# A new static order of steps for the five engines in the Layers phase of an attention and feed-forward kernel

## The reference, cut to what matters

```
h = shift_token(x)                      # half of the features come from the token before
q, k, v = split(h @ wqkv)               # 8 heads of 64
q, k = rotary_xpos(l2norm(q) * qs, l2norm(k) * ksc)
o = softmax(q k^T * 8, own and previous window of 128 keys, causal) v
x = x + o @ wo
h = layernorm(shift_token(x)) * lg + lb
a, g = split(h @ w1 + b1);  x = x + (a * gelu(g)) @ w2 + b2
```

## Time and profile before

| | before |
|---|---|
| median of three runs | 3927.06 us |
| the profiled execution | 3927.97 us |
| its span, first to last instruction | 3926.1 us |
| PE busy | 3360.0 us (86%) |
| DVE busy | 2846.7 us (73%) |
| ACT busy | 2352.7 us (60%) |
| POOL busy | 1511.6 us (39%) |
| mean granted TensorE clock | 0.953 of full speed |

### The profile page before, as it was taken

One profiled execution on the slowest core, in us unless ns is written; L12 is line 12 of the kernel. 1 busy time (PEld: TensorE's weight loads), 2 busy tenths in 40 slices (PEclk: granted clock), 3 DMA queues, 4 the chain that ended last, 5 costly groups with the idle time before them and its releaser, 6 DMA issues.

```text
span 3926.1 us, 77200 instructions
## 1 busy us (share of the span) xinstructions
PE 3360.0 (86%) x29600; PEld 1960.8 (50%) x29600; DVE 2846.7 (73%) x4121; ACT 2352.7 (60%) x2813; POOL 1511.6 (39%) x1171
## 2 busy tenths in 40 slices
PE   2888888888855799998999989878999899998998
PEld 1223232323223566565666666545656666665665
DVE  4778787777745777777777776667877777777764
ACT  0566666565643566666656666555666666666654
POOL 1212121212104445455444554443545544455443
PEclk7999999999987899999999999988999999999999
DMA  2222222222211000000000001010010100101000
GB/s 56 49 61 54 60 53 60 52 60 52 51 50 39 15 20 19 27 19 29 19 20 26 25 23 36 30 44 24 25 32 24 35 29 24 32 29 36 24 27 30
DMA packets 149008, 139.11 MB, mean 35 GB/s; under 512 B 11132, under 2 KB 147376, under 8 KB 148912
## 3 DMA queue, kind: packets, MB, share of 16 engines
q1 hardware_dynamic: 148912, 137.78, 13.4%
HBM read 70.40 MB, written 33.55 MB: 26 GB/s over the span
## 4 chain that ended last, share of the span: by engine, by line
PE 35%; DVE 15%; ACT 11%; issue 7%; POOL 1%; DMA 1%; SPq 0%; DVEq 0%; ACTq 0%; POOLq 0%
PE f_p L1026 13%; PE f_p L1162 7%; DVE f_Ph L1374 6%; PE f_p L1133 5%; PE f_p L1052 3%; PE f_p L1043 3%; ACT f_Ph L1253 2%; ACT f_Pl L1245 2%; DVE f_xh L1456 2%; PE f_p L1059 2%; ACT f_hT L1274 1%; DVE f_rt L248 1%; ACT f_gates L1268 1%; DVE f_xT_l L1343 1%; PE f_p L1008 1%
## 5 line engine op out<-in xcount | busy, mean ns | idle before, releaser
L654 DVE TENSOR_REDUCE m_negm<-m_p 128x2 f16<-128x1024 f32 x512 | 608.7, 1222 | 169.2 <-PE m_p L473 167.5
L576 ACT ACTIVATE m_Pr<-m_p 128x1024 f32<-128x1024 f32 x512 | 500.4, 1020 | 164.0 <-PE m_p L492 159.6
L1374 DVE TENSOR_TENSOR f_Ph<-f_Pl,f_Ph 128x896 f16<-128x896 f32 x256 | 377.0, 1514 | 213.3 <-ACT f_Ph L1253 213.3
L1540 POOL TENSOR_TENSOR f_u<-f_u,f_bt 128x1024 f32<-128x1024 f32 x128 | 301.8, 2358 | 465.6 <-DVE f_bt L1359 465.6
L1556 POOL TENSOR_TENSOR f_hT<-f_gates,f_hT 128x512 f16<-128x512 f32 x192 | 234.2, 1223 | 587.9 <-ACT f_gates L1276 587.6
L1268 ACT ACTIVATE f_gates<-f_p,f_bias 128x512 f32<-128x512 f32 x192 | 131.4, 684 | 469.0 <-PE f_p L1162 469.0
L501 PE MATMUL m_o<-m_Pr,m_vm 128*32 128x512 f32 x2048 | 341.6, 646 | 13.0 <-ACT m_Pr L576 13.0
L1026 PE MATMUL f_p<-f_wq_h,f_xT_h 128*128 128x512 f16 x768 | 307.0, 400 | 26.1 <-DVE f_xhT_l L1462 12.7
L1545 POOL TENSOR_TENSOR f_u<-f_u,f_rn 128x1024 f32<-128x1024 f32 x128 | 289.1, 2258 | 74.3 <-DVE f_mark_v L1387 74.3
L1392 DVE TENSOR_REDUCE f_negm<-f_p 128x4 bf16<-128x1024 f32 x256 | 300.8, 1222 | 17.0 <-PE f_p L1059 16.6
L1026 PE MATMUL f_p<-f_wq_l,f_xT_h 128*128 128x512 f16 x768 | 305.3, 398 | 0.0
(11 more groups left out here) (235 smaller groups left out, 8540.8 us busy)
## 6 DMA issues: line engine op xcount, KB each, us to landing
f_xs<-out SPq DMA_DIRECT2D x32, 512.0 KB, 4.4
f_xr<-out SPq DMA_DIRECT2D x32, 512.0 KB, 5.0
out<-f_xb SPq DMA_DIRECT2D x32, 512.0 KB, 3.0
m_xin<-in_L_attn_x SPq DMA_DIRECT2D x16, 512.0 KB, 4.1
out<-m_xn SPq DMA_DIRECT2D x16, 512.0 KB, 3.0
m_QT<-m_hi SPq DMA_DIRECT2D x128, 64.0 KB
m_KT<-m_hi SPq DMA_DIRECT2D x128, 64.0 KB
m_xr<-in_L_attn_x SPq DMA_DIRECT2D x16, 512.0 KB, 4.7
```

The source lines that it names most:

```text
L576: act.activation(Pr[kt % 2][:, 2 * u:2 * u + 2, :].rearrange("p h t -> p (h t)"), psum[w.slot("M2", g, kt, u)][:, :], ACT.Exp).then_inc(*w ...
L654: dve.tensor_reduce(negm[:, t, pr // 2, :, pr % 2], psum[w.slot("M1", h, u)][:, :].rearrange("p (a k) -> p a k", a=2), AX.X, ALU.max, nega ...
L1374: dve.tensor_tensor(Pp[h % 4][:, 1, :], Pl[h % 2][:], Pp[h % 4][:, 0, :], ALU.subtract).then_inc(*p_lo_ready.up(I))
L1540: pool.tensor_tensor(u[t][:], u[t][:], bt[:], ALU.add).then_inc(*bt_used.up(I))
```

## The change

The change rewrites the table and nothing else: every engine has the instructions that it had, SP's queue stays the same, and PE's, ACT's, DVE's and POOL's steps are in another order.

```diff
     order = {
-        "PE": """... C.ST,3 A.QK,3 D.WO,0 C.L1,0
-               D.WO,1 D.WO,2 D.WO,3 C.L1,1 F.W1,0 ...
+        "PE": """... C.ST,3 A.QK,3 C.L1,0 D.WO,0
+               D.WO,1 D.WO,2 D.WO,3 C.L1,1 F.W1,0 ...
         "ACT":
-               F.H1,0 F.W1,2 F.H1,1 F.W1,3 C.LM F.H1,2 F.W1,4 F.H1,3 F.W1,5 F.H1,4 F.H1,5 C.L2,0 C.PH,0 ...
+               F.H1,0 F.W1,2 F.H1,1 F.W1,3 F.H1,2 C.LM F.W1,4 F.H1,3 F.W1,5 F.H1,4 C.L2,0 F.H1,5 C.PH,0 ...
         "DVE":
-               ... A.QK,2 A.QK,3 D.WO,0 D.WO,1 D.WO,2 C.L1,0 D.WO,3 C.L1,1
-               F.W1,0 C.L1,2 F.W1,1 C.L1,3 C.LM F.W1,2 A.RN F.W1,3 F.W1,4 F.W1,5 F.ZB N.LN F.W2,0 C.PL,0 C.PL,1 F.W2,1 F.W2,2 N.LA
-               C.PL,2 C.PV,0 C.PL,3 C.PV,1 N.XH C.PV,2 C.PV,3""",
+               ... A.QK,2 C.L1,0 A.QK,3 D.WO,0 D.WO,1 D.WO,2 D.WO,3 C.L1,1
+               F.W1,0 C.L1,2 F.W1,1 C.L1,3 F.W1,2 C.LM F.W1,3 N.LN F.W1,4 A.RN F.W1,5 F.ZB F.W2,0 F.W2,1 C.PL,0 C.PL,1 F.W2,2 N.LA
+               C.PL,2 C.PV,0 C.PV,1 C.PL,3 N.XH C.PV,2 C.PV,3""",
-        "POOL": """A.QK,0 ... A.QK,3 F.H1,0 F.H1,1 F.H1,2 F.H1,3 F.H1,4 F.H1,5 A.NM,0 N.LR A.SQ,0 A.SH,0 A.NM,1 ... A.NM,3 A.SQ,3 A.SH,3 N.LS""",
+        "POOL": """A.QK,0 A.QK,1 A.QK,2 F.H1,0 F.H1,1 A.QK,3 F.H1,2 F.H1,3 A.NM,0 F.H1,4 F.H1,5 N.LR A.SQ,0 A.SH,0 A.NM,1 ... A.NM,3 N.LS A.SQ,3 A.SH,3""",
```

More of the change, by code:

```diff
@@ L798, in layers_phase @@
     order = {
-        "PE": """C.V,0 C.V,1 C.V,2 C.V,3 A.XT C.ST,0 D.OT,0 D.OT,1 A.QK,0 C.ST,1 A.QK,1 C.ST,2 A.QK,2 C.ST,3 A.QK,3 D.WO,0 C.L1,0
+        "PE": """C.V,0 C.V,1 C.V,2 C.V,3 A.XT C.ST,0 D.OT,0 D.OT,1 A.QK,0 C.ST,1 A.QK,1 C.ST,2 A.QK,2 C.ST,3 A.QK,3 C.L1,0 D.WO,0
                D.WO,1 D.WO,2 D.WO,3 C.L1,1 F.W1,0 C.L1,2 F.W1,1 C.L1,3 F.W1,2 F.W1,3 C.LM F.W1,4 F.W1,5 C.L2,0 F.W2,0 F.W2,1 C.L2,1
@@ L802, in layers_phase @@
         "ACT": """C.V,0 C.V,1 C.V,2 C.V,3 A.XT C.ST,0 D.OT,0 D.OT,1 A.QK,0 C.ST,1 A.QK,1 C.ST,2 A.QK,2 C.ST,3 A.QK,3 F.W1,0 F.W1,1
-               F.H1,0 F.W1,2 F.H1,1 F.W1,3 C.LM F.H1,2 F.W1,4 F.H1,3 F.W1,5 F.H1,4 F.H1,5 C.L2,0 C.PH,0 A.HI,0 C.L2,1 C.PH,1 C.L2,2
+               F.H1,0 F.W1,2 F.H1,1 F.W1,3 F.H1,2 C.LM F.W1,4 F.H1,3 F.W1,5 F.H1,4 C.L2,0 F.H1,5 C.PH,0 A.HI,0 C.L2,1 C.PH,1 C.L2,2
                C.PH,2 A.HI,1 C.L2,3 C.PH,3 N.XH A.HI,2 A.HI,3""",
-        "DVE": """C.V,0 C.V,1 C.V,2 C.V,3 A.XT D.OT,0 D.OT,1 A.QK,0 A.QK,1 A.QK,2 A.QK,3 D.WO,0 D.WO,1 D.WO,2 C.L1,0 D.WO,3 C.L1,1
-               F.W1,0 C.L1,2 F.W1,1 C.L1,3 C.LM F.W1,2 A.RN F.W1,3 F.W1,4 F.W1,5 F.ZB N.LN F.W2,0 C.PL,0 C.PL,1 F.W2,1 F.W2,2 N.LA
-               C.PL,2 C.PV,0 C.PL,3 C.PV,1 N.XH C.PV,2 C.PV,3""",
-        "POOL": """A.QK,0 A.QK,1 A.QK,2 A.QK,3 F.H1,0 F.H1,1 F.H1,2 F.H1,3 F.H1,4 F.H1,5 A.NM,0 N.LR A.SQ,0 A.SH,0 A.NM,1 A.SQ,1 A.SH,1
-               A.NM,2 A.SQ,2 A.SH,2 A.NM,3 A.SQ,3 A.SH,3 N.LS""",
-        "SP": """A.XT N.LX C.XR F.W2,0 F.W2,1 F.W2,2 N.XH""",
+        "DVE": """C.V,0 C.V,1 C.V,2 C.V,3 A.XT D.OT,0 D.OT,1 A.QK,0 A.QK,1 A.QK,2 C.L1,0 A.QK,3 D.WO,0 D.WO,1 D.WO,2 D.WO,3 C.L1,1
+               F.W1,0 C.L1,2 F.W1,1 C.L1,3 F.W1,2 C.LM F.W1,3 N.LN F.W1,4 A.RN F.W1,5 F.ZB F.W2,0 F.W2,1 C.PL,0 C.PL,1 F.W2,2 N.LA
+               C.PL,2 C.PV,0 C.PV,1 C.PL,3 N.XH C.PV,2 C.PV,3""",
+        "POOL": """A.QK,0 A.QK,1 A.QK,2 F.H1,0 F.H1,1 A.QK,3 F.H1,2 F.H1,3 A.NM,0 F.H1,4 F.H1,5 N.LR A.SQ,0 A.SH,0 A.NM,1 A.SQ,1 A.SH,1
+               A.NM,2 A.SQ,2 A.SH,2 A.NM,3 N.LS A.SQ,3 A.SH,3""",
+        "SP": """A.XT F.W2,0 N.LX C.XR F.W2,1 F.W2,2 N.XH""",
     }
```

## The result

| | before | changed |
|---|---|---|
| median of the runs | 3926.84 us | 3965.28 us (3958.99 to 3968.09) |
| ratio to before, with its interval | | 1.0097 [1.0081, 1.0113] |
| span of the profiled execution | 3926.1 us | 3963.0 us |
| PE busy | 3360.0 us | 3382.9 us |
| mean granted clock of TensorE | 0.953 | 0.941 |

A forecast was written before the change was run, and what follows sets the result against it. PE was taken as the bound, busy 74.48 of 81 us in a round. Over 13 loop rounds per layer, +0.2 (layer 0) and +1.0 (layer 1) sum to 15.6 us on 3927.1: 3943 us, range 3908 to 3975.

The forecast's parts named there:

- the likeliest case: Whole kernel: the prediction's own forecast, 3935 to 3955 us, chance 0.35.
- The unrolled rounds I take at 0: Rounds outside the two 13-round loops: no change in time, 0 us.
- the front: Round's start: `L1,0` before `WO,0` on PE, before `QK,3` and `WO` on DVE; cost 0.
- The clock, -0.2 per round: Turn of the round: low-clock stretch stays put and half the delay within it is given back, -0.2 us.
- rival D: PE's waits before the turn: clock falls more often or longer, 22 us, 3965 us; chance 0.12.
- `V,0` behind `PV,3`, +0.72: Round's end: next round's `V,0` waits for `PV,3`'s division instead of `XH`'s drain, +0.72 us per round.
- the last pair: Last two `PL` instructions of a round on DVE: in layer 0 end 0.3 us earlier, still split by `NM,2`.
- Layer 0's path, +0.42: Layer 0 loop rounds before the clock term: last `PL` pair -0.3 and `V,0` +0.72 us per round.
- Layer 1, +1.22 before the clock: Layer 1 loop rounds: `ZB` kept out, delaying the last `PL` pair +0.5 us, plus `V,0` +0.72.
- The waits of 0.55 and 1.45: PE's waits before `L2,0` and `L2,3`: the 0.55 us goes, the 1.45 us shrinks.
- PE's busy time should not change: PE over the whole kernel: same instructions, so busy time stays the same.

The follow-up runs named there:

- e3: Changed kernel with only `LN` put back behind `W1,5` and `ZB` on DVE: 3946.13 us, ratio 1.0050.
- e8: Kernel before with only `LN` moved forward on DVE, to behind `W1,3`: 3962.52 us, ratio 1.0086.
- e5: Changed kernel with `PV,2` given PSUM slot p0 and `PV,3` the other one: 3952.26 us, ratio 1.0060.
- e17: Changed kernel with 8 extra matmuls on PE ahead of `PV,2`: 3948.49 us, ratio 1.0052.
- e13: Kernel before with 16 extra matmuls on PE ahead of `PV,2`: 3911.12 us, ratio 0.9957.
- e6: Changed kernel with the front and `LN` both put back to their old order: 3907.34 us, ratio 0.9943.
- e12: Kernel before with `LN` early; meant to move `W2`'s drain too, but no instruction moved, so e8 repeated: 3962.52 us, ratio 1.0088.
- e15: Kernel before with `LN` early and 16 extra matmuls on PE ahead of `PV,2`: 3949.92 us, ratio 1.0053.
- e18: Kernel before with the new front alone and 16 extra matmuls on PE ahead of `PV,2`: 3976.88 us, ratio 1.0128.

## Why the prediction was right and wrong

Slower was forecast, and slower it is. 3965 lies between 3908 and 3975, but not in the 3935 to 3955 of the likeliest case: the change is 38 us where 16 were forecast. Point by point, the step that failed first:

- **"The unrolled rounds I take at 0": the step that failed.** They lost 13.7 us. The prediction's walk through the round gave `LN` nothing, neither its own time nor a wait: `RN`, which now stands behind it, was forecast at 2072.2, +18.7 of the round, and starts at +20.5. It took `LN`'s inputs as ready. The copy of `x1` takes some 16 us from its issue; `LN` used to come some 20 us after it, and now comes before it has landed. Outside the loops the waits for it are 16.5 us instead of 2.5, and PE passes them on (10.54 and 4.58 at `W2`). In the loops 26 of them, 50.5 us in all, make no round longer beside the new front (e3: 81.91 and 81.92 without them), though the chain that ended last in the changed kernel gives this copy 11% of the span. e3, which gives back 19 us, shows that `LN`'s place is the cause. That it is the transfer and not the 2.0 us of `LN` in front of a gate product is not separated: no run brings the copy earlier, and in e8's loops `LN`'s place costs 0.85 per round without any such wait.
- **The clock, -0.2 per round: wrong sign.** It was taken that the stretch stays where it is and gives half of a delay back. Measured: it costs 81.91 - 80.81 = 1.10 in layer 0 where it cost 0.70, and about 81.92 - 81.53 = 0.39 in layer 1 where it cost 0.30. That is +0.40 and +0.09, because it now reaches further into the turn, in every other round of layer 0 and one in four of layer 1. This is rival D in kind, at under a third of its price: 13 x 0.49 = 6.4 us of its 22. That D's figure, 3965, is the measured one is luck, since D had the unrolled rounds at 0 as well.
- **`V,0` behind `PV,3`, +0.72: right in layer 0.** 2.97 us after the first instruction behind the last pair were forecast, 2.96 are there, and the wait is for L1405 (1.29, forecast 1.4). Undo only this, by the slot (e5), and layer 0's round falls by 1.1; layer 1's stays within 0.06, with 6.8 us of a round at half clock instead of 4.3 (layer 0: 7.3 instead of 6.0).
- **Layer 0's path, +0.42: right, in part by luck.** e17 against e13, in rounds at full clock, show 80.81 - 80.37 = +0.44. But the last pair, forecast 0.3 earlier, ends where it did (+47.26 against +47.20); it is again 3.97 long beside an `NM` of 2.75. `V,0` starts at +50.15 instead of +49.37, and what was forecast at 0, the front, gives 0.35 back: from `V,0` to the next `x1` sum it is 30.65 instead of 31.00.
- **Layer 1, +1.22 before the clock: too high.** `ZB` is kept out as forecast (2.36), and the last pair ends 0.8 later (+48.00 against +47.22, forecast 0.5). The full-clock rounds of e17 in layer 1 have 81.53 to 81.61 against a mean of 80.78 in e13, about +0.75, for here too the front gives something back.
- The waits of 0.55 and 1.45 are gone, as forecast or more. "PE's busy time should not change" was wrong by 22.9 us, for the clock's sake.

The sum with the measured terms, over the 13 rounds of each loop: path 13 x (0.44 + 0.75) = 15.5, clock 13 x (0.40 + 0.09) = 6.4, outside 13.7, in all 35.6, against 36.9 of span. For path and clock this makes 21.9, where 23.2 were measured and 15.6 forecast; the difference of 1.3 lies in the first rounds of a loop, which are not yet like the others (83.88 in layer 1).

What stays open: the parts don't add up (the front and `LN` cost 39 and 38 one by one in e6, 58 together), and which wait brings a stretch at half clock was not settled. e8's, e12's and the changed kernel's rounds are all within 0.06 of 81.92 though their orders differ, and three rounds in four of the kernel before have a stretch while e13's have none; no run was made that explains the common length.

## What to carry to other kernels

When an instruction is moved up, look up when each of its inputs lands, transfers too, and compare with the time between issue and use before; do it in the unrolled rounds as well, where nothing hides a wait. Ask of a stretch at low clock what follows it: ahead of a wait it was nearly free here (0.09 us), where PE was dense it cost almost half of its length (1.57 of 3.4). And before a shuffle of many steps is judged, look for the one drain that can be moved into a gap: here `PV,1`, ahead of the blocked pair, is worth 17 us by itself.

## What the hardware showed that was not expected

- A stretch of 3.4 us at half clock cost 0.09 us at one place of a round (e15) and 1.57 at another (e18).
- 16 useless matmuls, 1.75 us of PE's time per round, made the kernel before 18 us faster, ratio 0.9957 [0.9943, 0.9970], by holding the clock at full speed in every loop round (mean over the span 0.962 against 0.953).
- The shifted copy of `x1` lands some 16 us after its first issue, a fifth of a round; its second part, three rows of 512 bytes (L1625), alone has 11.21 us on SP's queue.
